# A fused decoder layer on one core: the shared expert's last 64 gates and ups computed as one product of 128 columns, and its down taken over 64 partitions

## The chip, the cores and the metric

The kernel runs on one core of one Trainium2 chip. The metric is the time of one execution on the device in microseconds. Times are given as the median of several executions. A second source is one profiled execution, whose trace names each instruction with its engine, its line in the kernel, its start and its duration. TensorE appears in the rows as PE (its weight loads as PEld), VectorE as DVE, ScalarE as ACT, GpSimd as POOL and SyncE, which issues most transfers, as SP.

## The reference, cut to what matters

One decoder layer over 8 sequences of 112 tokens (896 tokens) of width 512: causal self-attention, cross-attention to 375 context rows, and a feed-forward block, each on layer-normalised input and added to the residual. The change is in the last block:

```python
logits = x @ gate_w.T                       # 8 experts
probs = softmax(logits); top 2 of 8, normalised -> combine
g_sh = x @ shared_gate.T                    # I_SH = 2 * 352 = 704
u_sh = x @ shared_up.T
out = silu(g_sh) * u_sh @ shared_down.T     # shared expert, every token
g = einsum('nh,eih->nei', x, expert_gate)   # routed experts, I = 352
u = einsum('nh,eih->nei', x, expert_up)
y = einsum('nei,ehi->neh', silu(g) * u, expert_down)
out = out + einsum('neh,ne->nh', y, combine)
```

## The kernel before

**Numbers.** Every float32 product is done as three products of a 32-bit type that TensorE takes at full rate (fp32r): each operand is split into a high part (a ScalarE copy, `hi`) and a low part (source minus high part, mostly on VectorE, `low`), and `mm3` issues high by high, low by high and high by low (lines 512 to 514).

**The shared expert.** Its 704 hidden channels are padded to 768 and done in `NS = 6` chunks of 128; the last chunk holds 64 real channels and 64 of zeros. The tokens are done in two halves of `HT = 448`. For half `n` and chunk `c`, `up_pe(n, c, 0)` computes the gates and `up_pe(n, c, 1)` the ups, transposed (channels in the partitions, tokens in the columns): 4 contraction steps of 3 matmuls each, 448 columns, into a bank of PSUM. ScalarE applies silu to the gates into `sg` (`up_silu`), VectorE multiplies by the ups in PSUM (`up_mul`), ScalarE makes the high part of the result (`up_hi`, `hs`), VectorE the low part (`up_low`). The down contracts over the 128 channels of a chunk: for each of four tiles of 112 tokens, 3 matmuls of 512 columns.

**First half.** It runs on from the cross-attention: chunks 0 to 5 with `down_pe(c)`, which accumulates in four banks over all chunks. The weights of a chunk (1024 columns of gates and ups, 512 of the down) are loaded to `sf` and split in thirds (`s_hi_act(c, p)`, `s_low(c, p)`) into a ring of three buffers. Beside it VectorE works out the routing in a long row of small instructions. Its written order around the change is: `up_low(0, 3)`, `s_low(5, 0)`, `s_low(5, 1)`, normalised rows (`rows_normal`), `up_mul(0, 4)`, the experts' numbers, `up_low(0, 4)`, `s_low(5, 2)`, `up_mul(0, 5)`, `up_low(0, 5)`. TensorE's order is `up_pe(0, 5, 0)`, `up_pe(0, 5, 1)`, `down_pe(4)`, `down_pe(5)`.

**Second half and routed experts.** These are jobs: three shared jobs of two chunks each (0 and 1, 2 and 3, 4 and 5), and then 14 jobs of routed experts, which together have 21 blocks of 128 gathered rows. A job's weights come to a buffer `F[k % 2]`, and are split into `E[k % 2]`, part by part (`part_hi`, `part_low`), once the down of job `k - 2` has read that buffer. The down of a shared job is computed one job later: in the third job TensorE's order is `up_pe(1, 4, 0)`, `up_pe(1, 4, 1)`, the transposes of the first expert block (`turn_x`), the second job's down, `up_pe(1, 5, 0)`, `up_pe(1, 5, 1)`. The first expert block follows: `expert_up(0, 0)` (gates, 12 matmuls of 352 columns), the third job's down, `turn_x`, `expert_up(0, 1)`. In the shared down each of 4 token tiles gets 3 matmuls for the even chunk and 3 for the odd one.

In the third job VectorE's order is `up_mul(1, 4)`, the addition of the second job's result to the residual, `up_low(1, 4)`, the low part of the turned rows, the low parts of the first expert's gates and ups (`E_lo`, three parts), `up_mul(1, 5)`, `up_low(1, 5)`. ScalarE goes in the corresponding order.

Result banks of the gates and ups are handed out by a list of uses (`ups`), over four banks in rotation; `gu_wait` waits for the reader of the use before it in the same bank.

The tail: each expert block's result is added to the output by an indirect DMA of GpSimd, which waits for those of the job before.

Of the kernel before, what the change touches and what calls it, by code (L numbers as in the profile page):

```python
# [32 lines left out]
ISQ = 1.0 / float(DH) ** 0.5  # L33
LNE = 1e-5
SC = KC * 256 + D
NRB = -(-NT // BS)


# [42 lines left out]
def decoder_layer(nc, x_d, ctx_d, wqk_d, wv_d, wo_d, wqx_d, wkv_d, gw_d, moe_d, wexp_d, ident_d, mask_d, cst_d,  # L81
                  out_d):
    stack = ExitStack()
    with stack:
# [253 lines left out]

        def piece(k):

            last = (3, WU, WU + SC)
            if jobs[k][0] == "s":
                return (0, 0, SC), last
            return (0, 0, 940), (1, 940, 1880), (2, 1880, WU), last

        ups = [("u", 0, c, a) for c in range(4) for a in range(2)] + ["R"]
        ups += [("u", 0, c, a) for c in range(4, NS) for a in range(2)]
        t_uses, y_uses = [], []
        for n, (kind, j, k, _) in enumerate(its):
            prev = its[n - 1] if n else None  # L350
            ups += [("b", j, a) for a in range(2)] if kind == "e" else [("u", 1, 2 * j + q, a) for q in range(2) for a in range(2)]
# [98 lines left out]
        half_set = sig("half_set", [0])  # L450
        gl_done, lg_done = sig("gl_done", range(NB)), sig("lg_done", range(NB))

        third = [(c, p) for c in range(NS) for p in range(3)]
        s_hi, s_lo = sig("s_hi", third), sig("s_lo", third)
        g0_kept, u0_kept = sig("g0_kept", [0]), sig("u0_kept", [0])
        gu_full = sig("gu_full", ups)
# [51 lines left out]
        def tensor(e):  # L508
# [252 lines left out]
            def gu_wait(u):  # L761
                v = gu_before[u]
                if v[0] == "kn":
                    w.wait_ge(*kn_done[v[1]])
                elif v[0] == "oo":
                    w.wait_ge(*oo_done[v[1]])
                elif v[0] == "tx":
                    tx_free(v[1])
                elif v == "R":
                    w.wait_ge(*gu_dve["R"])  # L770
                elif v[:3] == ("u", 0, 0):
                    w.wait_ge(*(u0_kept if v[3] else g0_kept)[0])
                elif v[-1] == 0:
                    w.wait_ge(*gu_act[v[:-1]])
                else:
                    w.wait_ge(*gu_dve[v[:-1]])

            def up_pe(n, c, a):
                u, o = ("u", n, c, a), 0
                if n:  # L780
                    k = at_job["s", c // 2]
                    p, o = E[k % 2], WU if c % 2 else 0
                    part_wait(k, 3 if c % 2 else 0)
                else:
                    p = ring[c % 3] if c else SE
                    w.wait_ge(*s_lo[c, 1])
                w.wait_ge(*xT_done[3][4 * n + 3])
                gu_wait(u)
                for k in range(KC):
                    i = mm3(GU[u][:, 0:HT], at(p, ALL, toks(o + k * 256 + a * 128, 128)), at(xT, ALL, k, toks(n * HT, HT)),  # L790
                            k == 0, k == KC - 1)
                i.then_inc(*gu_full.did(u))

            def down_pe(c, tiles=range(4)):
                p = ring[c % 3] if c else SE
                w.wait_ge(*h_lo[0, c])
                w.wait_ge(*s_lo[c, 2])
                for b in tiles:
                    if c == 0:
                        if b == 1:  # L800
                            tx_free(tx_last[3])
                        else:
                            w.wait_ge(*x_exped[NK - 1, b])
                    i = mm3(AC[b][0:T, :], at(hs[c % 2], ALL, toks(b * T, T)), at(p, ALL, toks(1024, D)), c == 0, c == NS - 1)
                    i.then_inc(*ac_full.did((0, c, b)))

            def part_wait(k, p):
# [43 lines left out]
            def job_down(kind, j):  # L851
                k = job_of[j] if kind == "e" else at_job[kind, j]
                p = E[k % 2]
                if kind == "e":
                    u = (kind, j)
                    part_wait(k, 3)
                    w.wait_ge(*ht_lo[j])
                    y_wait(u)
                    for i, (o, n) in enumerate(IC):
                        z = WU + i * D  # L860
                        t = mm3(YB[u][:, :], (hT[j % 2][0][0:n, i, :], hT[j % 2][1][0:n, i, :]),
                                (p[0][0:n, z:z + D], p[1][0:n, z:z + D]), i == 0, i == 2)
                    t.then_inc(*y_full.did(u))
                    return
                w.wait_ge(*h_lo[1, 2 * j + 1])
                for t in range(4):
                    u = (kind, j, t)
                    y_wait(u)
                    for q in range(2):
                        i = mm3(YB[u][0:T, :], at(hs1 if q else hs[0], ALL, toks(t * T, T)), at(p, ALL, toks((WU if q else 0) + 1024, D)),  # L870
                                q == 0, q == 1)
                    i.then_inc(*y_full.did(u))

            def job_pe(n):
                kind, j, k, _ = its[n]
                prev = its[n - 1][0:2] if n else None
                nxt = its[n + 1] if n + 1 < len(its) else (None, 0)
                if kind == "e":
                    expert_up(j, 0)
                else:  # L880
                    up_pe(1, 2 * j, 0)
                if prev and prev[0] == "e":
                    turn_h(prev[1])
                elif prev and kind == "e":
                    job_down(*prev)
                if kind == "s":
                    up_pe(1, 2 * j, 1)
                    if k == 0:
                        up_pe(1, 2 * j + 1, 0)
                if nxt[0] == "e":  # L890
                    turn_x(nxt[1])
                if kind == "e":
                    expert_up(j, 1)
                if prev and (prev[0] == "e" or kind == "s"):
                    job_down(*prev)
                if kind == "s":
                    if k:
                        up_pe(1, 2 * j + 1, 0)
                    up_pe(1, 2 * j + 1, 1)

            last = NH // 2 - 1
            rows_pe(*keys[0])
# [45 lines left out]
            e.matmul(GU["R"][0:T, 64:72], tab[:, T:2 * T], small["cum"][:, 64:72], start=True, stop=True).then_inc(*gu_full.did("R"))  # L948
            down_pe(2, (2, 1))
            for c in (4, 5):  # L950
                for a in range(2):
                    up_pe(0, c, a)
                down_pe(c - 1)
            down_pe(NS - 1)
# [8 lines left out]
        def scalar(e):  # L963
# [243 lines left out]
            def up_silu(n, c):  # L1207
# [8 lines left out]
                elif n:  # L1216
                    w.wait_ge(*gu_dve[("u", 1, c - 2) if c > 1 else ("u", 0, NS - 1)])
                s_ = sg1 if n and c % 2 else sg[c % 2]
                silu(("u", n, c), ("u", n, c, 0), s_[:, :])

            def up_hi(n, c):
# [9 lines left out]
                hi(to[0][:, :], h_[:, :]).then_inc(*h_hi.did((n, c)))  # L1231

            def part_hi(k, p):
                for n, a, b in piece(k):
# [104 lines left out]
            s_hi_act(4, 2)  # L1339
            up_silu(0, 3)  # L1340
            s_hi_act(5, 0)
            s_hi_act(5, 1)
            up_hi(0, 3)
            s_hi_act(5, 2)
            part_hi(0, 0)
            up_silu(0, 4)
            up_hi(0, 4)
# [8 lines left out]
        def vector(e):  # L1356
# [264 lines left out]
                return (sg1, hh1, hs1) if n and c % 2 else (sg[c % 2], hh[c % 2], hs[c % 2])  # L1621

            def up_mul(n, c):
                g, h_ = ("u", n, c, 1), bufs(n, c)
                w.wait_ge(*gu_act["u", n, c])
                w.wait_ge(*gu_full[g])
                if n == 0 and c == 0:
                    w.wait_ge(*u0_kept[0])
                    e.tensor_tensor(h_[1][:, :], h_[0][:, :], h_[1][:, :], ALU.mult).then_inc(*gu_dve.did(("u", n, c)))
                    return  # L1630
                e.tensor_tensor(h_[1][:, :], h_[0][:, :], GU[g][:, 0:HT], ALU.mult).then_inc(*gu_dve.did(("u", n, c)))

            def up_low(n, c):
                h_ = bufs(n, c)
                w.wait_ge(*h_hi[n, c])
                low(h_[2][1][:, :], h_[1][:, :], h_[2][0][:, :]).then_inc(*h_lo.did((n, c)))

            def part_low(k, p):
                for n, a, b in piece(k):
# [221 lines left out]
            rows_normal(1)  # L1861
            up_low(0, 3)
            s_low(5, 0)
            s_low(5, 1)
            rows_normal(2)
            rows_normal(3)
            for b in range(4, NB):
# [11 lines left out]
            do(e.tensor_reduce(small["le2"][0:1, 0:NSL], le, X, ALU.add))  # L1879
            e.tensor_scalar(eid[:, :], small["le2"][0:1, 0:NSL], float(NE - 1), None, ALU.min).then_inc(*eid_done.did(0))  # L1880
            up_low(0, 4)
            s_low(5, 2)
            up_mul(0, 5)
            up_low(0, 5)
            part_low(0, 0)
# [128 lines left out]
        def sync(e):  # L2014
# [76 lines left out]
            def sf_load(c):  # L2091
                k = c - 2 if c > 3 else 0 if c == 1 else None
                if k is not None:
                    w.wait_ge(*s_lo[k, 2])
                e.dma_start((sf_e if c < 2 else sf[c % 2])[:, :], moe_d[c]).then_inc(*sf_in[c % 2].did(c))

            for n in range(4, NB * MC):
                ctx_load(n)
# [12 lines left out]
            def part_load(k, p):  # L2111
# [5 lines left out]
                        if (n == 3) == (p == 3):  # L2117
                            w.wait_ge(*e_lo[k - 2, n])
                elif k:
                    w.wait_ge(*s_lo[5, 2])  # L2120
                to = (Fd_in if p == 3 else Fu_in)[k % 2]
                if kind == "s":
                    o = WU if p == 3 else 0
                    e.dma_start(F[k % 2][:, o:o + SC], moe_d[2 * j + (p == 3)]).then_inc(*to.did(k))
# [115 lines left out]
```

## Time and profile before

| | |
|---|---|
| median of 3 runs | 971.27 us (970.53 to 971.85) |
| the profiled execution | 970.31 us |
| its span, first to last instruction | 968.50 us |
| TensorE busy | 927.6 us, 96% of the span |
| VectorE, ScalarE, GpSimd busy | 550.7, 455.3, 178.3 us |

An engine's busy share is an average over the whole span. What is idle and what ended the idle time is told by the timeline, in which an entry has square brackets if the engine sat idle before it. Matmuls are pipelined: an entry's duration is longer than the distance to the next one, and the distance is the cost in a saturated stretch.

### The profile page before, as it was taken

Reading aid. Unit: us, or ns where it says so; the run is one execution under the profiler, and the core shown is the slowest. Engines: PE = TensorE matmul, PEld = TensorE weight load, DVE = VectorE, ACT = ScalarE, POOL = GpSimd, SP = SyncE. Lnnn points to the kernel's source line nnn. Section 1 sums busy time; section 2 is a strip of 40 time slices with the busy share of each in tenths; the row PEclk is TensorE's granted clock in tenths of the full one; section 3 lists DMA queues with packets and bytes.
Section 4 is the critical chain, followed back from the end, with each engine's and each line's share of the span. In section 5 each row is a group of like instructions: output and inputs, shape, how many; then the busy total and the mean of one; then the engine's idle time right before and its main releaser. Section 6 shows DMA issues by size and latency. Waiting matters only on the chain.

```text
span 968.5 us, 17911 instructions
## 1 busy us (share of the span) xinstructions
PE 927.6 (96%) x7250; PEld 806.7 (83%) x7250; DVE 550.7 (57%) x1192; ACT 455.3 (47%) x1113; POOL 178.3 (18%) x137
## 2 busy tenths in 40 slices
PE   4999999999999999989999999999999999999994
PEld 3999999999999999867777777777778888899994
DVE  6254444444444445575645646555457756888882
ACT  3342424232323233536666656666575224665651
POOL 1220202020202022501011011011000710222222
PEclk9999999999999999999999999999999999999998
DMA  5110541010202003222201010010032684999983
GB/s 189 67 44 22 178 149 66 23 66 22 66 23 66 22 22 110 65 58 75 65 24 24 11 33 23 13 33 13 1 126 77 237 252 171 324 295 283 303 201 44
DMA packets 31329, 94.12 MB, mean 97 GB/s; under 512 B 6176, under 2 KB 9488, under 8 KB 29328
## 3 DMA queue, kind: packets, MB, share of 16 engines
q1 hardware_dynamic: 26944, 83.80, 25.7%
q0 software_dynamic: 4304, 9.19, 5.0%
q8 instruction: 57, 0.93, 0.4%
q14 instruction: 24, 0.20, 0.1%
HBM read 74.33 MB, written 16.81 MB: 94 GB/s over the span
## 4 chain that ended last, share of the span: by engine, by line
PE 89%; DVE 4%; ACT 3%; issue 1%; DMA 1%; POOL 1%; SPq 0%; DVEq 0%; ACTq 0%; POOLq 0%
PE bank L512 24%; PE bank L513 23%; PE bank L514 23%; PE bank L709 5%; PE bank L726 4%; PE bank L584 3%; PE bank L559 3%; PE bank L676 1%; ACT ee L1129 1%; PE bank L571 1%; PE bank L736 1%; PE bank L822 1%; PE bank L600 1%; DVE E_lo L1360 1%; DVE rt L1370 1%
## 5 line engine op out<-in xcount | busy, mean ns | idle before, releaser
L1129 ACT ACTIVATE ee<-bank 125x448 f32<-125x448 f32 x192 | 91.2, 549 | 21.2 <-PE bank L709 20.2
L512 PE MATMUL bank<-xT_hi,wqk_hi 128*128 128x448 f32 x256 | 95.6, 374 | 1.4 <-DVE xT_lo L1360 1.4
L514 PE MATMUL bank<-xT_lo,wqk_hi 128*128 128x448 f32 x256 | 93.4, 365 | 0.0
L513 PE MATMUL bank<-xT_hi,wqk_lo 128*128 128x448 f32 x256 | 93.3, 365 | 0.0
L512 PE MATMUL bank<-wkv_hi,ctx_hi 128*125 128x512 f32 x192 | 80.3, 418 | 3.0 <-DVE kn L1512 1.5
L1360 DVE TENSOR_TENSOR E_lo<-F,E_hi 128x940 fp32r<-128x940 f32 (+2 forms) x62 | 80.8, 1330 | 1.6 <-ACT E_hi L967 1.5
L513 PE MATMUL bank<-wkv_hi,ctx_lo 128*125 128x512 f32 x192 | 76.1, 396 | 0.0
L514 PE MATMUL bank<-wkv_lo,ctx_hi 128*125 128x512 f32 x192 | 75.7, 394 | 0.0
L512 PE MATMUL bank<-wv_hi,xT_hi 128*112 128x256 f32 x256 | 72.2, 282 | 0.0
L513 PE MATMUL bank<-wv_hi,xT_lo 128*112 128x256 f32 x256 | 71.7, 280 | 0.0
L514 PE MATMUL bank<-wv_lo,xT_hi 128*112 128x256 f32 x256 | 71.6, 280 | 0.0
L1903 POOL TENSOR_TENSOR ctx_lo<-ctx_f,ctx_hi 128x500 fp32r<-128x500 f32 x24 | 30.4, 1269 | 222.4 <-ACT ctx_hi L967 222.4
L1442 DVE TENSOR_TENSOR xa<-xa,bank 128x512 f32<-128x512 f32 x56 | 38.4, 687 | 53.3 <-PE bank L514 53.3
L967 ACT ACTIVATE E_hi<-F 128x940 fp32r<-128x940 f32 (+2 forms) x62 | 67.8, 1148 | 0.9
L2005 POOL DMA_INDIRECT out<-yg,meta x21 | 38.9, 1854 | 144.6 <-DMA out<-yg,meta 80.1
L1903 POOL TENSOR_TENSOR wqk_lo<-wqk_f,wqk_hi 128x1024 fp32r<-128x1024 f32 x16 | 37.8, 2360 | 145.8 <-ACT wqk_hi L967 145.8
L967 ACT ACTIVATE qk<-bank 128x448 f32<-128x448 f32 x32 | 17.4, 545 | 97.7 <-PE bank L514 97.7
L1026 ACT ACTIVATE pp<-sm,nm 112x112 f32<-112x112 f32 x128 | 48.1, 377 | 30.2 <-DVE nm L1414 30.2
L1521 DVE COPY kT<-bank 128x250 f32<-128x250 f32 x48 | 20.0, 416 | 68.8 <-PE bank L676 68.7
L512 PE MATMUL bank<-E_hi,xgT_hi 128*128 128x352 f32 x168 | 56.3, 335 | 0.6 <-DVE E_lo L1360 0.6
L1109 ACT ACTIVATE sq<-bank 125x256 f32<-125x256 f32 (+1 forms) x64 | 24.6, 384 | 63.3 <-PE bank L514 63.3
L514 PE MATMUL bank<-E_lo,xgT_hi 128*128 128x352 f32 x168 | 54.1, 322 | 0.0
(323 smaller groups left out, 2406.8 us busy)
## 6 DMA issues: line engine op xcount, KB each, us to landing
F<-wexp SPq DMA_DIRECT2D x14, 1408.0 KB, 8.1
F<-wexp SPq DMA_DIRECT2D x14, 768.0 KB, 7.4
wqk_f<-wqk SPq DMA_DIRECT2D x16, 512.0 KB, 3.3
ctx_f<-ctx SPq DMA_DIRECT2D x24, 250.0 KB, 2.7
slots<-zt SPq DMA_DIRECT2D x1, 5397.0 KB, 19.6
xg<-slots SPq DMA_DIRECT2D x21, 256.0 KB, 7.9
F<-moe SPq DMA_DIRECT2D x6, 768.0 KB, 7.7
wv_f<-wv SPq DMA_DIRECT2D x8, 512.0 KB, 3.6
```

The lines of the kernel that those rows point to most:

```text
L512: e.matmul(out, a[0], b[0], start=first, stop=False)
L513: e.matmul(out, a[1], b[0], start=False, stop=False)
L514: return e.matmul(out, a[0], b[1], start=False, stop=last)
L709: i = e.matmul(SX[r][0:MS, g * 2 * T:(g + 1) * 2 * T], kT[n % 6][32 * r:32 * r + 32, g, :], qT[u % 2][32 * r:32 * r + 32, g, :, :], start= ...
L726: i = e.matmul(AB[32 * c:32 * c + VW, r * T:(r + 1) * T], vb[n % 6][:, 8 * (c // 2) + 2 * r + c % 2, :], ee[(4 * n + r) % 8][:, c * T:(c + ...
L967: return e.activation(out, src, ACT.Copy)
L1026: i = e.activation(pp[g][:, c, :], sm[g][:, c, :], ACT.Exp, bias=nm[g][:, c:c + 1], scale=ISQ, accum_out=rs[g][:, c:c + 1])
L1129: e.activation(ee[(4 * n + r) % 8][:, :], SX[r][0:MS, 0:4 * T], ACT.Exp, scale=0.25).then_inc(*x_exped.did((n, r)))
L1360: return e.tensor_tensor(out, src, high.bitcast(F32), ALU.subtract)
L1442: e.tensor_tensor(xa[:, j, :], xa[:, j, :], PJ[u][:, :], ALU.add).then_inc(*pj_dve.did(u))
L1903: return e.tensor_tensor(out, src, high.bitcast(F32), ALU.subtract)
L2005: e.indirect_dma_start(out_d, bass.IndirectOffsetOnAxis(ap=meta[:, unit_of[j], 0:1].bitcast(U32), axis=0), yg[j % 4][:, :], None, compute_ ...
```

## The change

Chunk 5 has 64 gates and 64 ups. They are now one product: gates in result partitions 0 to 63, ups in 64 to 127. Silu reads the lower partitions and writes the upper ones of `sg`, and the product with the ups, the high and the low part work on partitions 64 to 127 alone. The down contracts over the upper 64 partitions. The weights of the chunk are 1024 columns in place of 1536, loaded and split in two parts in place of three. So `up_pe(0, 5, 1)` and `up_pe(1, 5, 1)` are gone, with one `s_hi_act` and one `s_low`, and `up_hi(0, 3)` stands before the second `s_hi_act` of chunk 5.

```diff
+LAST = 2 * D
-            last = (3, WU, WU + SC)
+            last = (3, WU, WU + (LAST if k == 2 else SC))
...
-        ups += [("u", 0, c, a) for c in range(4, NS) for a in range(2)]
+        ups += [("u", 0, 4, 0), ("u", 0, 4, 1), ("u", 0, 5, 0)]
...
-        third = [(c, p) for c in range(NS) for p in range(3)]
+        third = [(c, p) for c in range(NS) for p in range(3 if c < NS - 1 else 2)]
+        down_third = [2] * (NS - 1) + [1]
+        low_rows = slice(64, 128)
...
                 for k in range(KC):
-                    i = mm3(GU[u][:, 0:HT], at(p, ALL, toks(o + k * 256 + a * 128, 128)), at(xT, ALL, k, toks(n * HT, HT)),
-                            k == 0, k == KC - 1)
+                    z = o + (k * 128 if c == NS - 1 else k * 256 + a * 128)
+                    i = mm3(GU[u][:, 0:HT], at(p, ALL, toks(z, 128)), at(xT, ALL, k, toks(n * HT, HT)), k == 0, k == KC - 1)
...
-                w.wait_ge(*s_lo[c, 2])
+                w.wait_ge(*s_lo[c, down_third[c]])
+                part, z = (low_rows, D) if c == NS - 1 else (ALL, 1024)
...
-                    i = mm3(AC[b][0:T, :], at(hs[c % 2], ALL, toks(b * T, T)), at(p, ALL, toks(1024, D)), c == 0, c == NS - 1)
+                    i = mm3(AC[b][0:T, :], at(hs[c % 2], part, toks(b * T, T)), at(p, part, toks(z, D)), c == 0, c == NS - 1)
...
                     for q in range(2):
-                        i = mm3(YB[u][0:T, :], at(hs1 if q else hs[0], ALL, toks(t * T, T)), at(p, ALL, toks((WU if q else 0) + 1024, D)),
-                                q == 0, q == 1)
+                        part, z = (low_rows, D) if 2 * j + q == NS - 1 else (ALL, 1024)
+                        i = mm3(YB[u][0:T, :], at(hs1 if q else hs[0], part, toks(t * T, T)),
+                                at(p, part, toks((WU if q else 0) + z, D)), q == 0, q == 1)
...
-                    up_pe(1, 2 * j + 1, 1)
+                    if k < 2:
+                        up_pe(1, 2 * j + 1, 1)
...
-                for a in range(2):
+                for a in range(2 if c == 4 else 1):
                     up_pe(0, c, a)
                 down_pe(c - 1)
...
+                if c == NS - 1:
+                    g = "u", n, c, 0
+                    w.wait_ge(*gu_full[g])
+                    e.activation(s_[low_rows, :], GU[g][0:64, 0:HT], ACT.Silu).then_inc(*gu_act.did(("u", n, c)))
+                    return
...
             s_hi_act(5, 0)
+            up_hi(0, 3)
             s_hi_act(5, 1)
-            up_hi(0, 3)
-            s_hi_act(5, 2)
...
-                e.tensor_tensor(h_[1][:, :], h_[0][:, :], GU[g][:, 0:HT], ALU.mult).then_inc(*gu_dve.did(("u", n, c)))
+                e.tensor_tensor(h_[1][part, :], h_[0][part, :], GU[g][part, 0:HT], ALU.mult).then_inc(*gu_dve.did(("u", n, c)))
...
             s_low(5, 0)
-            s_low(5, 1)
...
             up_low(0, 4)
-            s_low(5, 2)
+            s_low(5, 1)
...
-                    w.wait_ge(*s_lo[5, 2])
+                    w.wait_ge(*s_lo[5, 1])
```

The transfers of chunk 5 are cut to `LAST` columns in both halves, and the host packs the weights accordingly.

## Rows read from the trace of the kernel before

**Rows 1.** The page: busy time, share of the span and number of instructions.

```profile
PE 927.6 (96%) x7250; PEld 806.7 (83%) x7250; DVE 550.7 (57%) x1192; ACT 455.3 (47%) x1113; POOL 178.3 (18%) x137
```

**Rows 2.** Busy time by stretches; the last three columns are granted clock, DMA share, GB/s.

```profile
758.30:766.20 7.90, 7.90 (x37) 6.40 (x36) 7.04 (x13) 1.95 (x3) 6.58 (x6) 1.00 0.78 219
766.20:802.40 36.20, 36.20 (x173) 31.30 (x173) 19.53 (x25) 10.31 (x13) 8.85 (x10) 1.00 0.89 304
824.10:953.60 129.50, 129.44 (x766) 120.18 (x767) 105.61 (x126) 74.31 (x104) 35.85 (x19) 1.00 0.88 264
```

**Rows 3.** Timeline of TensorE, first token half: start, duration in us, instruction.

```profile
755.88 0.36 PE L512 MATMUL bank<-xT_hi,S2hi 128*128 128x448 f32 x1
...
758.31 0.36 PE L512 MATMUL bank<-xT_hi,S2hi 128*128 128x448 f32 x1
...
760.74 0.39 PE L512 MATMUL bank<-S1hi,hs0hi 128*112 128x512 f32 x1
```

**Rows 4.** Timeline of VectorE, the same stretch.

```profile
752.69 1.29 DVE L1360 TENSOR_TENSOR S2lo<-sf,S2hi 128x512 fp32r<-128x512 f32 x2
753.90 2.83 DVE L1767 TENSOR_SCALAR rows<-xs,mv,rstd 112x512 f32<-112x512 f32 x6
...
759.76 0.60 DVE L1360 TENSOR_TENSOR hs0lo<-sg,hs0hi 128x448 fp32r<-128x448 f32 x1
760.29 0.67 DVE L1360 TENSOR_TENSOR S2lo<-sf,S2hi 128x512 fp32r<-128x512 f32 x1
...
762.27 0.63 DVE L1360 TENSOR_TENSOR hs_slo<-hh_s,hs_shi 128x448 fp32r<-128x448 f32 x1 [0.65 <-ACT hs_shi L967]
```

**Rows 5.** The chain that ended last, from the second shared job's down on.

```profile
802.71 0.58 ACT hs0hi L967
...
803.77 0.89 ACT E_hi L967
804.68 3.24 DVE E_lo L1360 x3
```

**Rows 6.** Timeline of TensorE where the routed experts begin.

```profile
808.12 0.40 PE L512 MATMUL bank<-E_hi,xgT_hi 128*128 128x352 f32 x1 [0.58 <-DVE E_lo L1360]
808.36 0.32 PE L513 MATMUL bank<-E_hi,xgT_lo 128*128 128x352 f32 x1
```

**Rows 7.** Timeline of TensorE, cross-attention scores over 32 partitions, opened at several points.

```profile
717.61 1.04 PE L709 MATMUL bank<-qT,kT 32*125 32x224 f32 x16
...
717.90 0.74 PE L709 MATMUL bank<-qT,kT 32*125 32x224 f32 x12
...
718.09 0.56 PE L709 MATMUL bank<-qT,kT 32*125 32x224 f32 x8
...
718.28 0.37 PE L709 MATMUL bank<-qT,kT 32*125 32x224 f32 x4
718.58 0.22 PE L512 MATMUL bank<-xT_hi,gw_hi 128*8 128x112 f32 x1
```

**Rows 8.** Timeline of TensorE, an expert's down over 96 partitions.

```profile
825.63 0.40 PE L512 MATMUL bank<-E_hi,hT0hi 96*128 96x512 f32 x1
...
826.33 0.32 PE L512 MATMUL bank<-E_hi,xgT_hi 128*128 128x352 f32 x1
```

**Rows 9.** Busy time by stretches after the last matmul; columns as in rows 2.

```profile
957.55:959.00 1.45, 0.00 (x1) 0.00 (x0) 0.75 (x1) 0.00 (x0) 0.00 (x0) 1.00 0.86 151
...
959.50:960.00 0.50, 0.00 (x0) 0.00 (x0) 0.00 (x0) 0.00 (x0) 0.00 (x0) 0.69 0.00 0
```

**Rows 10.** Timeline of TensorE at the first projection.

```profile
18.96 0.72 PE L512 MATMUL bank<-xT_hi,wqk_hi 128*128 128x448 f32 x1
...
20.60 0.57 PE L513 MATMUL bank<-xT_hi,wqk_lo 128*128 128x448 f32 x1
20.97 0.41 PE L514 MATMUL bank<-xT_lo,wqk_hi 128*128 128x448 f32 x1
```

More of the change, by code:

```diff
@@ L350, in decoder_layer @@
             prev = its[n - 1] if n else None
-            ups += [("b", j, a) for a in range(2)] if kind == "e" else [("u", 1, 2 * j + q, a) for q in range(2) for a in range(2)]
+            ups += [("b", j, a) for a in range(2)] if kind == "e" else [("u", 1, 2 * j + q, a) for q in range(2) for a in range(2) if 2 * j + q + a < NS]
             if prev and prev[0] == "e":
@@ L772, in gu_wait @@
                     w.wait_ge(*(u0_kept if v[3] else g0_kept)[0])
-                elif v[-1] == 0:
+                elif v[-1] == 0 and v[2:3] != (NS - 1,):
                     w.wait_ge(*gu_act[v[:-1]])
@@ L785, in up_pe @@
                     p = ring[c % 3] if c else SE
-                    w.wait_ge(*s_lo[c, 1])
+                    w.wait_ge(*s_lo[c, down_third[c] - 1])
                 w.wait_ge(*xT_done[3][4 * n + 3])
@@ L1230, in up_hi @@
                 h_, to = (hh1, hs1) if n and j else (hh[j], hs[j])
-                hi(to[0][:, :], h_[:, :]).then_inc(*h_hi.did((n, c)))
+                part = low_rows if c == NS - 1 else ALL
+                hi(to[0][part, :], h_[part, :]).then_inc(*h_hi.did((n, c)))
             def part_hi(k, p):
@@ L1623, in up_mul @@
             def up_mul(n, c):
-                g, h_ = ("u", n, c, 1), bufs(n, c)
+                g, h_ = ("u", n, c, 1 if c < NS - 1 else 0), bufs(n, c)
+                part = low_rows if c == NS - 1 else ALL
                 w.wait_ge(*gu_act["u", n, c])
@@ L1635, in up_low @@
                 w.wait_ge(*h_hi[n, c])
-                low(h_[2][1][:, :], h_[1][:, :], h_[2][0][:, :]).then_inc(*h_lo.did((n, c)))
+                part = low_rows if c == NS - 1 else ALL
+                low(h_[2][1][part, :], h_[1][part, :], h_[2][0][part, :]).then_inc(*h_lo.did((n, c)))
             def part_low(k, p):
@@ L2094, in sf_load @@
                     w.wait_ge(*s_lo[k, 2])
-                e.dma_start((sf_e if c < 2 else sf[c % 2])[:, :], moe_d[c]).then_inc(*sf_in[c % 2].did(c))
+                z = LAST if c == NS - 1 else SC
+                e.dma_start((sf_e if c < 2 else sf[c % 2])[:, 0:z], moe_d[c, :, 0:z]).then_inc(*sf_in[c % 2].did(c))
             for n in range(4, NB * MC):
@@ L2123, in part_load @@
                     o = WU if p == 3 else 0
-                    e.dma_start(F[k % 2][:, o:o + SC], moe_d[2 * j + (p == 3)]).then_inc(*to.did(k))
+                    z = LAST if k == 2 and p == 3 else SC
+                    e.dma_start(F[k % 2][:, o:o + z], moe_d[2 * j + (p == 3), :, 0:z]).then_inc(*to.did(k))
                 else:
@@ L2208 @@
     gw = inner(L0_ffn_gate_w)
-    up = np.zeros((2, NS * 128, D), np.float32)
-    up[0, :2 * NI] = np.asarray(L0_ffn_shared_gate)
-    up[1, :2 * NI] = np.asarray(L0_ffn_shared_up)
-    dn = np.zeros((NS * 128, D), np.float32)
-    dn[:2 * NI] = np.asarray(L0_ffn_shared_down).T
-    upc = inner(up.reshape(2, NS, 128, D).transpose(1, 0, 2, 3).reshape(NS, 256, D)).reshape(NS, 128, KC * 256)
-    moe = np.concatenate([upc, dn.reshape(NS, 128, D)], axis=2)
+    full = (NS - 1) * 128
+    up = np.stack([np.asarray(L0_ffn_shared_gate), np.asarray(L0_ffn_shared_up)])
+    dn = np.asarray(L0_ffn_shared_down).T
+    upc = inner(up[:, :full].reshape(2, NS - 1, 128, D).transpose(1, 0, 2, 3).reshape(NS - 1, 256, D)).reshape(NS - 1, 128, KC * 256)
+    moe = np.zeros((NS, 128, SC), np.float32)
+    moe[:NS - 1] = np.concatenate([upc, dn[:full].reshape(NS - 1, 128, D)], axis=2)
+    moe[NS - 1, :, :D] = inner(up[:, full:].reshape(128, D)).reshape(128, KC * 128)
+    moe[NS - 1, 64:, D:LAST] = dn[full:]
     eup = inner(np.concatenate([np.asarray(L0_ffn_expert_gate), np.asarray(L0_ffn_expert_up)], axis=1))
```

## The prediction, as made before the changed kernel ran

> **What bounds the kernel now.** I read the page first: TensorE is busy for 927.6 of 968.5 us [rows 1]. An average says nothing of one stage, so next came the busy time by stretches [rows 2]. From 758.3 to 802.4 us (the end of the first token half of the shared expert and two jobs of the second) TensorE is busy all the time, and so it is from 824.1 to 953.6. Between lies the passage from shared to routed experts, where it isn't. So a matmul saved in a saturated stretch shows only if what comes next is ready by then. Therefore I went to the two places where the change takes matmuls away, and read what the next TensorE instruction needs.
>
> One product of a chunk (12 matmuls of 448 columns) takes 758.31 - 755.88 = 2.43 us [rows 3], 0.20 each.
>
> **First token half: a product less.** The change removes product (5, ups) of tokens 0 to 447, at 758.31 to 760.74, straight before the down of chunk 4 [rows 3]. That down waits for `h_lo[0, 4]`. Its writer on VectorE starts at 759.76 and takes 0.60, so it ends at 760.36, only 0.38 us ahead of the down [rows 4]. Hence TensorE is free at 758.31 but VectorE sets the pace. VectorE works in program order from 752.7 on without an idle entry in these rows; what the change takes out ahead of that instruction is one of two `s_low` of chunk 5: 753.90 - 752.69 = 1.21 for the two, so 0.60 for one [rows 4]. New end 759.76. I add 0.15 from the end of the low part to the first matmul (in the row at 808.12 it is 0.20: the low parts end at 804.68 + 3.24 = 807.92 [rows 5, 6]) and 0.08 because a first matmul after a wait is longer (0.40 against 0.32 [rows 6]). The down of chunk 4 effectively starts at 759.99 instead of 760.74: a gain of 0.75, not 2.43; 1.6 us become a stall of TensorE.
>
> Its 12 matmuls of 512 columns take 12 x 0.233 = 2.80 us (three take 826.33 - 825.63 = 0.70 [rows 8]), until 762.8. The down of chunk 5 needs `h_lo[0, 5]`, before at 762.27 + 0.63 = 762.90 [rows 4]. Its chain (one `s_low`, the product with the ups, ScalarE's cast, the low part) is led by the same VectorE queue, so it moves by 0.60 to 762.3: no second stall, with 0.5 us of cover. Should that cover fail, each 0.1 us costs 0.1.
>
> **Second token half: a product less.** The change removes the last product of the third shared job, which ended in the stretch before 808.12. There TensorE is already waiting, 0.58 us, for VectorE's `E_lo` [rows 6]. The chain [rows 5] says for what: when the down of the second job ends (802.7), ScalarE casts `hs0hi`, `xgT_hi` and then the first expert's weight parts, and VectorE makes their low parts until 807.9. That expert's buffer is the one which the second job's down has just read, so the chain starts at the end of that down and at nothing else: 5.4 us whatever TensorE does meanwhile. TensorE used to cover it with two products; now it has one. The stall grows from 0.58 by 2.43 to about 3.0 us, and the second saving is worth 0. The down of the third job also keeps its place, since the product with the ups stands behind those low parts on VectorE.
>
> **Downs over 64 partitions.** Four tiles in the first half, four in the second, three matmuls each; column counts stay, so does the time for streaming. The trace has no such 64-partition matmul. Two rows bound what entering and leaving it costs. 96 partitions, same type: 0.70 us for three, as with 128, cost 0 [rows 8]. 32 partitions at offsets 0 to 96 [rows 7]: the first four matmuls take 717.90 - 717.61 = 0.29, the next four 718.09 - 717.90 = 0.19, so entry costs 0.10; the last four take 718.58 - 718.28 = 0.30, so leaving costs 0.11. The new matmul begins at partition 64, an offset that the 96-partition rows don't have and the 32-partition ones do, so I take 0.10. In the first half the four 64-partition tiles stand together: 2 changes. In the second each tile is a 128-partition group followed by a 64-partition one: 8 changes. 10 x 0.10 = 1.0 us, all in stretches that TensorE sets; bounds 0 and 10 x 0.2 = 2.0 (twice the row, for a load that isn't hidden either).
>
> The Trainium skill (TensorEngine Tiling (Array Packing), "Key Properties") states that changing the tiling mode drains the engine. It speaks against this change; by it the term above is real, without it zero, and rows 7 agree with it to the extent of those tenths. That page gives no time for it.
>
> **At nothing.** Elementwise work on the upper partitions has the same length per partition, so the same time. 256 KB less for chunk 5 in each half, one ScalarE cast less and shorter parts of job 2: all under TensorE's saturated stretch [rows 2]; VectorE's share in the first half is counted above. One use less in the ring of result banks shifts banks by one, and each use still waits for one that is four uses back. SyncE's load of job 1 waits for the low part that ends 0.6 earlier; nothing waits for it. `up_hi(0, 3)` now stands before the second cast, which no longer waits for a down; ScalarE's next work that somebody awaits is microseconds later. From 824.1 on everything shifts with TensorE.
>
> **Sum.** -0.75 + 0 + 1.0 = +0.25 us. Against the profiled execution (970.31: span 968.50 and 1.81 around it) that is 970.6; the median of the runs shown is 0.96 above that execution, so 971.5. About 0.2% (1.9 us) is what this kernel's measurement can tell from no change.
>
> **Rivals.**
> *No price for the 64 partitions.* For it: the 96-partition rows. Then -0.75: 970.5.
> *The clock falls in the longer stall (the slower side).* After the last matmul the granted clock is 1.00 in 957.55 to 959.00 and 0.69 in 959.50 to 960.00 [rows 9], the step from 2.4 to 1.2 GHz some 2 us after TensorE stopped, and TensorE had been idle once shortly before. A stall of 3.0 us is longer than that, though full work stands ahead of it. At the slow level a 448-column matmul takes 0.37 (20.97 - 20.60) instead of 0.20, from 18.96 to at least 20.97 [rows 10]: a loss of 1.0 us on 2 us of slow work. If the slow stretch is twice that, 2.0; if it lasted over the expert product and the whole third down (7.5 us), some 7. I take 2.0, for 971.27 + 0.25 + 2.0 = 973.5. It decides once the stall is long enough for the step; against it: the stall at 808 of 0.58 is far too short to show anything, and 3.0 is only just beyond the 2 us.
> The Trainium skill (TensorE: Matmul & The Clock Gate, "What's actually happening") says that the slow level is the default and activity lifts it; by that rule this rival would happen once the stall counts as idle.
> *Both products are saved in full.* 2 x 2.43 = 4.9: 966.4. That needs VectorE's chains to be no bound; rows 4 to 6 speak against it.
> *The DMA tail.* The last add to the output follows TensorE's end with transfers of some us; if they fall differently, +-1.5.
>
> **Chances.** Forecast (gain 0.75, changes of mode about 1.0) 0.42; no price 0.25; clock 0.18; both in full 0.05; tail or something else 0.10, split evenly. Faster by over 0.2% (below 969.3): 0.05 + a part of the tail, 0.07. Slower (above 973.2): most of the clock case and a part of the rest, 0.17. Within: 0.76. The range from 970.0 to 973.8 holds the first three cases with their bounds (0 to 2.0 for the mode, 1.0 to 2.2 for the clock) and leaves out the full saving and the long slow stretch. For the likeliest case alone 970.5 to 972.5.
>
> **What would show it.** Right: a TensorE wait of about 1.5 us before the down of chunk 4, released by `hs0lo`; a wait of about 3.0 before the first 128x352 product, released by `E_lo`, which still ends 5.2 us after the second job's down; the third down some 0.8 us longer than before at the same granted clock. Wrong: a third down as long as before (no price); a clock row below 1.00 after 805 us; or low parts of the expert's weights that don't follow the down, which would free the second product. The prediction goes wrong most easily in the size of the mode changes, as no row has this form, and in the clock.

## The result, and the profile of the changed kernel

The changed kernel is slower: 973.68 us (median of 9, 971.56 to 974.26) against 970.58 (median of 9) before, a ratio of 1.0029 with a 95% interval from 1.0018 to 1.0039, +3.1 us. The forecast was 971.5 with no measurable change; the measured time lies at the upper end of the range, where the rival with the falling clock had put it (973.5). The forecast was built on the median of 971.27 then known for the kernel before, 0.7 above the 970.58 of all nine executions; measured against that kernel, the upper end of the range was +2.5 us and the result is +3.1. The profiled execution took 973.01 with a span of 971.2.

The page's line of busy times answers to [rows 1]:

```profile
PE 927.3 (95%) x7226; PEld 803.6 (83%) x7226; DVE 549.1 (57%) x1191; ACT 454.1 (47%) x1112; POOL 180.1 (19%) x137
```

There are 24 matmuls fewer, and the engine's busy time is the same: what remained has become longer. Two lines of TensorE's waits from 700 us on (releaser: us in total, times, longest):

```profile
PE bank L516 <- DVE E_lo L1372: 4.6, 3, 3.0
PE bank L516 <- issue: 2.5, 2, 1.3
```

The first holds the wait of 3.0 us forecast before the first expert product. The second has one of 1.3 before the down of chunk 4; the profile names no releaser for it ("issue"), not `hs0lo` as forecast, and a reordering below tests what it waits for. Both stand in the timeline of TensorE, and with them what the engine does on resuming:

```profile
759.89 0.48 PE L516 MATMUL bank<-S1hi,hs0hi 128*112 128x512 f32 x1 [1.32 <-issue]
...
807.80 0.63 PE L516 MATMUL bank<-E_hi,xgT_hi 128*128 128x352 f32 x1 [3.04 <-DVE E_lo L1372]
808.23 0.50 PE L517 MATMUL bank<-E_hi,xgT_lo 128*128 128x352 f32 x1
808.52 0.50 PE L518 MATMUL bank<-E_lo,xgT_hi 128*128 128x352 f32 x1
...
810.58 0.40 PE L516 MATMUL bank<-E_hi,xgT_hi 128*128 128x352 f32 x1
810.81 0.32 PE L517 MATMUL bank<-E_hi,xgT_lo 128*128 128x352 f32 x1
```

From 808.2 to 810.6 the 352-column matmuls are 0.29 to 0.30 us apart and last 0.50; before, they last 0.32 [rows 6]. The stretches tell why (columns as in [rows 2]):

```profile
806.00:807.00 1.00, 0.00 (x0) 0.00 (x0) 1.00 (x2) 0.61 (x2) 0.00 (x0) 1.00 0.00 0
807.00:807.80 0.80, 0.00 (x0) 0.03 (x1) 0.77 (x2) 0.00 (x0) 0.00 (x0) 0.68 0.03 10
807.80:810.60 2.80, 2.80 (x10) 2.80 (x11) 1.07 (x2) 0.57 (x1) 0.00 (x0) 0.50 0.47 105
810.60:811.10 0.50, 0.50 (x4) 0.50 (x4) 0.00 (x0) 0.00 (x0) 0.00 (x0) 0.90 0.76 315
811.10:818.10 7.00, 7.00 (x27) 3.49 (x25) 2.06 (x3) 0.00 (x0) 0.00 (x0) 1.00 0.68 252
```

The granted clock stands at 1.00 until 807.0, falls inside the wait (at about 807.3), is 0.50 (1.2 in place of 2.4 GHz) while the first expert product runs, and is back at 810.7. TensorE's last matmul before the wait had ended at 804.76. The product takes 811.13 - 807.80 = 3.33 us; before it took 810.12 - 808.12 = 2.00: +1.33.

At 811.1 the clock is full again, and the third job's down is still long. A 128-partition group, a 64-partition group, and the start of the next:

```profile
811.60 0.39 PE L518 MATMUL bank<-E_lo,hs0hi 128*112 128x512 f32 x1
811.92 0.48 PE L516 MATMUL bank<-E_hi,hs_hi 64*112 64x512 f32 x1
812.24 0.39 PE L517 MATMUL bank<-E_hi,hs_lo 64*112 64x512 f32 x1
812.48 0.39 PE L518 MATMUL bank<-E_lo,hs_hi 64*112 64x512 f32 x1
812.80 0.49 PE L516 MATMUL bank<-E_hi,hs0hi 128*112 128x512 f32 x1
...
818.09 0.66 PE L827 MATMUL bank<-ident,xg 128*128 128x128 f32 x4
```

A matmul of 512 columns elsewhere comes 0.23 after the one before it. Here the first after a change comes 0.32 later (811.60 to 811.92, 812.48 to 812.80), and the one behind it again 0.32 (811.92 to 812.24). So each change costs 2 x 0.09 = 0.18 us, once on the way in and once behind the first matmul. The down takes 818.09 - 811.13 = 6.96 us against 5.53 before (810.12 to 815.65): +1.43, eight changes.

The sum along TensorE's timeline, changed minus before (two single executions, which can differ by some tenths of a us before the change begins: the last matmul of chunk 5's product starts at 757.7 in one kernel's trace below and at 758.3 in another's): -0.44 at the first product of the second token half (765.83 against 766.27), -0.32 at the first expert product, +1.01 at the third down, +2.44 behind it, +2.83 at the last matmul (959.98 against 957.15).

### The profile page after: what moved, and what is told of

Read it like the earlier page. It is cut to its first block, busy times and chain, and to the rows that moved or that the text cites. A ratio compares the mean times of both kernels' runs of the same rounds, so it can differ in the third digit from the quotient of the medians.

```text
span 971.2 us, 17862 instructions
## 1 busy us (share of the span) xinstructions
PE 927.3 (95%) x7226; PEld 803.6 (83%) x7226; DVE 549.1 (57%) x1191; ACT 454.1 (47%) x1112; POOL 180.1 (19%) x137
## 4 chain that ended last, share of the span: by engine, by line
PE 89%; DVE 5%; ACT 3%; issue 1%; DMA 1%; POOL 1%; SPq 0%; DVEq 0%; ACTq 0%; POOLq 0%
PE bank L516 24%; PE bank L517 23%; PE bank L518 23%; PE bank L713 5%; PE bank L730 4%; PE bank L588 3%; PE bank L563 3%; PE bank L680 1%; ACT ee L1136 1%; PE bank L575 1%; PE bank L740 1%; PE bank L827 1%; PE bank L604 1%; DVE E_lo L1372 1%; DVE rt L1382 1%
## 5 line engine op out<-in xcount | busy, mean ns | idle before, releaser
L1372 DVE TENSOR_TENSOR E_lo<-F,E_hi 128x940 fp32r<-128x940 f32 (+3 forms) x62 | 80.2, 1320 | 1.7 <-issue 0.8
L974 ACT ACTIVATE E_hi<-F 128x940 fp32r<-128x940 f32 (+3 forms) x62 | 67.3, 1139 | 0.9
L517 PE MATMUL bank<-E_hi,xgT_lo 128*128 128x352 f32 x168 | 54.6, 325 | 0.0
```

The lines of the kernel that those rows point to most:

```text
L517: e.matmul(out, a[1], b[0], start=False, stop=False)
L974: return e.activation(out, src, ACT.Copy)
L1372: return e.tensor_tensor(out, src, high.bitcast(F32), ALU.subtract)
```

## The experiments

All are timed with 11 executions, or as many as named, beside the kernel before on the same chip. "Full downs" means: chunk 5's downs contract over all 128 partitions; the lower 64 rows of its weights are zeros, so the result stays. "Before" in brackets is the median of the kernel before in the same session.

**The four corners: mode changes and clock.** First the changed kernel with full downs.

```diff
-                part, z = (low_rows, D) if c == NS - 1 else (ALL, 1024)
+                part, z = (ALL, D) if c == NS - 1 else (ALL, 1024)
...
-                        part, z = (low_rows, D) if 2 * j + q == NS - 1 else (ALL, 1024)
+                        part, z = (ALL, D) if 2 * j + q == NS - 1 else (ALL, 1024)
```

> The change, but both downs of chunk 5 contract over all 128 partitions; the weights of the lower 64 are zeros, so the result is the same. Theory (three terms: the mode changes cost about 0.18 us each, the clock's fall 1.3, the first half gives 0.5 to 0.75 back): the third job's down goes from 6.96 us to about 5.5 and the first half's last down from 3.0 to 2.8; 1.8 us less than the changed kernel, about 971.9. The stall of 3.0 us and the fall of the clock stay. Rival (64-partition groups cost nothing, all of the loss is clock and stall): no difference, 973.7.

Then the changed kernel with the second half's product done twice, to keep TensorE at work; the first copy is thrown away.

```diff
                 gu_wait(u)
+                for k in range(4 if n and c == NS - 1 else 0):
+                    mm3(GU[u][:, 0:HT], at(p, ALL, toks(o + k * 128, 128)), at(xT, ALL, k, toks(n * HT, HT)), k == 0, k == 3)
                 for k in range(KC):
```

> The change, but the product of chunk 5 in the second half is done twice (the first copy is overwritten), so that TensorE works in place of the long stall. Theory: the stall shrinks to about 0.6 us, the granted clock stays at 1.00 behind it, the first expert product takes 2.0 us instead of 3.3, and the kernel is 1.3 faster than the changed one, about 972.3, with a smaller spread between runs. Rival (the work itself was needed late, the clock is only a symptom): no gain, or a loss of 2.4 for the added product, 976.

Both edits:

> Both edits together: downs of chunk 5 over 128 partitions, product of chunk 5 in the second half done twice. If the three terms add up: 1.8 + 1.3 = 3.1 us less than the changed kernel, about 970.4, that is 0.1 to 0.7 below the kernel before. Rival (the two overlap, since the clock's fall lies next to the down): only 1.8 less, 971.9.

And the changed kernel as it is, again, to have all corners:

> The changed kernel again, unaltered, so that it stands on the same chip and in the same rounds as its variants. If the three terms add up, its gap to the kernel before is that of the variant with 128-partition downs (0.8) plus the mode changes (1.8), about 2.6 us; the four corners (with and without each of the two edits) would then be +2.6, +0.8, +1.0 and -0.7, nearly additive. Rival (the terms overlap): under 2.0.

| | no work added in the stall | product done twice |
|---|---|---|
| downs over 64 partitions | 973.36 (before 970.46) | 971.30 (before 970.26) |
| full downs | 971.06 (before 970.26) | 969.52 (before 970.26) |

Against the kernel before: +2.9, +1.0, +0.8, -0.7. Full downs take off 1.8 with the stall filled and 2.1 with it open; filling it takes off 1.5 with full downs and 1.9 with 64-partition ones. The 95% interval of each ratio is about 0.9 us to either side, so +0.8 and -0.7 alone are hardly told from no change; the differences of 1.5 to 2.1 along each side are larger and agree in both rows and both columns. Both causes are real, and nearly additive. Two of the expectations were somewhat low: filling the stall of the changed kernel took off 1.9 (1.3 expected), and its own gap was 2.9 (2.6 expected). The timeline of TensorE with full downs, the stall open:

```profile
807.49 0.40 PE L516 MATMUL bank<-E_hi,xgT_hi 128*128 128x352 f32 x1 [3.05 <-DVE E_lo L1372]
...
810.85 0.59 PE L516 MATMUL bank<-E_hi,hs0hi 128*112 128x512 f32 x1
...
816.57 0.60 PE L827 MATMUL bank<-ident,xg 128*128 128x128 f32 x4
```

The slow product stays (3.36 us); the down is back at 5.72, of which the first matmuls are still slow: together 1.55 us more than before (2.00 and 5.53). The granted clock in this trace, and in that of the changed kernel's second session, which had a wait of 3.05 up to 807.83:

```profile
804.50:807.80 3.30, 0.31 (x2) 0.34 (x3) 3.27 (x4) 1.80 (x3) 0.00 (x0) 1.00 0.01 2
807.80:811.20 3.40, 3.40 (x13) 3.36 (x12) 0.76 (x2) 0.57 (x1) 0.00 (x0) 0.51 0.65 195
...
804.80:807.80 3.00, 0.00 (x0) 0.00 (x0) 2.97 (x4) 1.84 (x3) 0.00 (x0) 1.00 0.01 3
807.80:811.20 3.40, 3.37 (x12) 3.40 (x13) 1.10 (x2) 0.57 (x1) 0.00 (x0) 0.50 0.50 136
```

The clock is low for 3.4 us in both, as in the first trace (807.3 to 810.7), but here it falls only at the end of the wait (807.8 in the second session) or behind it: with full downs about 0.35 us after the matmuls had resumed at 807.49. In the first trace 0.5 us of the slow stretch lie in the wait, where they cost nothing. That is why the same stretch costs 1.33 there and 1.55 in these two (in the second session the product takes 3.55 and the down 6.94).

With 64-partition downs and the stall filled:

```profile
807.27 0.40 PE L516 MATMUL bank<-E_hi,xgT_hi 128*128 128x352 f32 x1 [0.58 <-DVE E_lo L1374]
...
809.27 0.44 PE L516 MATMUL bank<-E_hi,hs0hi 128*112 128x512 f32 x1
...
816.28 0.66 PE L829 MATMUL bank<-ident,xg 128*128 128x128 f32 x4
```

The other way round: the product takes 2.00, the down 7.01. It also shows that 12 matmuls more in front of the expert product don't delay it: it starts at 807.27 with them and at 807.80 without, and the two executions are 0.5 us apart already at the start of the down of chunk 4 (759.37 and 759.89). That is the second saving, worth 0.

**Half of the product done twice** (6 extra matmuls, full downs).

> 128-partition downs, and only half of the product of chunk 5 in the second half is done twice (6 matmuls more), so the stall is about 1.8 us. Theory (the clock falls only if TensorE stood still long enough, 2.5 us in the changed kernel's trace): no fall, the same time as with the whole product done twice, about 0.7 below the kernel before. Rival (any stall over about 1.5 us brings it in some of the runs): a spread over two levels 1.4 us apart, median between.

969.87 (before 970.46), -0.6 by the medians, but the ratio is 1.0000 (0.9991 to 1.0009), so no gain over the kernel before is shown. In the profiled execution the wait is 1.81 us and the product takes 2.00. Nine of the eleven executions lie between 969.34 and 970.35 with a mean granted clock of 0.996; two lie at 971.87 and 972.20 with 0.994. So the theory seems to hold for most executions and the rival for two of them (these two have no trace, so that their clock fell at this place is inferred): where the border lies is not settled, and whether the clock falls is not fixed by the kernel alone.

**Is it the number of partitions or their offset?** The kernel before, whose chunk 5 has its real channels in the lower 64 partitions, with the downs of that chunk over these alone.

```diff
+                    part = slice(0, 64) if c == NS - 1 else ALL
-                    i = mm3(AC[b][0:T, :], at(hs[c % 2], ALL, toks(b * T, T)), at(p, ALL, toks(1024, D)), c == 0, c == NS - 1)
+                    i = mm3(AC[b][0:T, :], at(hs[c % 2], part, toks(b * T, T)), at(p, part, toks(1024, D)), c == 0, c == NS - 1)
...
+                        part = slice(0, 64) if 2 * j + q == NS - 1 else ALL
-                        i = mm3(YB[u][0:T, :], at(hs1 if q else hs[0], ALL, toks(t * T, T)), at(p, ALL, toks((WU if q else 0) + 1024, D)),
+                        i = mm3(YB[u][0:T, :], at(hs1 if q else hs[0], part, toks(t * T, T)), at(p, part, toks((WU if q else 0) + 1024, D)),
```

> The kernel before, with one edit: the downs of chunk 5 contract over partitions 0 to 63 alone (the other 64 channels are the padding of zeros, so the result is the same). No work is removed from the products, nothing is reordered, the stall stays at 0.58 us. Theory (going from a 128-partition to a 64-partition group and back costs about 0.18 us each way, whatever the offset): the third down takes 6.95 us in place of 5.53, the first half's last down some 0.35 more, and the kernel is 1.8 us slower than before. Rival (only the offset of 64 costs; groups that begin at partition 0 are free like the 96-partition ones): no difference.

972.43 (before 970.58), +1.85, with the ratio between 1.0010 and 1.0028. The timeline of its TensorE in the third down:

```profile
811.33 0.39 PE L514 MATMUL bank<-E_lo,hs0hi 128*112 128x512 f32 x1
811.64 0.48 PE L512 MATMUL bank<-E_hi,hs_hi 64*112 64x512 f32 x1
811.97 0.40 PE L513 MATMUL bank<-E_hi,hs_lo 64*112 64x512 f32 x1
812.21 0.39 PE L514 MATMUL bank<-E_lo,hs_hi 64*112 64x512 f32 x1
812.53 0.48 PE L512 MATMUL bank<-E_hi,hs0hi 128*112 128x512 f32 x1
```

The same 0.31 to 0.33 us on each side of a change. The third down takes 6.92 us, against 6.96 with the groups at partition 64. The offset plays no part; the change of group size alone does, and it costs the whole 1.8 us without any stall or slow clock beside it.

**The first half's saving.** Full downs, and VectorE makes the operands of the two downs before the small instructions that number the experts.

```diff
             up_mul(0, 4)
+            up_low(0, 4)
+            s_low(5, 1)
+            up_mul(0, 5)
+            up_low(0, 5)
+            part_low(0, 0)
+            part_low(0, 3)
             le, le2 = (small[i][0:1, :].rearrange("p (j e) -> p j e", e=NE) for i in ("le", "le2"))
...
             e.tensor_scalar(eid[:, :], small["le2"][0:1, 0:NSL], float(NE - 1), None, ALU.min).then_inc(*eid_done.did(0))
-            up_low(0, 4)
-            s_low(5, 1)
-            up_mul(0, 5)
-            up_low(0, 5)
-            part_low(0, 0)
-            part_low(0, 3)
```

> Downs of chunk 5 over 128 partitions, and in the first half VectorE makes the operands of the downs of chunks 4 and 5 before the small instructions that number the experts. Theory (the first half's saving is lost to VectorE's order): TensorE goes on without the stall of 1.3 us before the down of chunk 4, and the kernel is 1.5 us faster than the one with downs over 128 partitions alone, about 970.4. Rival (something else, such as the weights' low parts or the second down's operand, takes the place of that wait): under 0.5 of it arrives.

The timeline of its TensorE, from the last matmul of chunk 5's product on:

```profile
758.12 0.36 PE L518 MATMUL bank<-xT_lo,S2hi 128*128 128x448 f32 x1
758.32 0.39 PE L516 MATMUL bank<-S1hi,hs0hi 128*112 128x512 f32 x1
...
761.17 0.49 PE L516 MATMUL bank<-S2hi,hs_shi 128*112 128x512 f32 x1
...
764.05 0.37 PE L516 MATMUL bank<-xT_hi,E_hi 128*128 128x448 f32 x1
```

No wait before the down of chunk 4; the second half starts at 764.05 instead of 765.65. In time: 969.81 against 971.06 with full downs alone, -1.25 of the 1.5 expected (no saving against the kernel before is shown by this alone: 0.9989 to 1.0007). VectorE's order was what kept the first saving.

In this kernel's profiled execution (968.34) the wait before the expert product was 3.05 us as before, and the clock did not fall:

```profile
803.00:806.00 3.00, 0.02 (x1) 0.00 (x0) 2.97 (x4) 1.88 (x3) 0.00 (x0) 1.00 0.01 3
806.00:808.00 2.00, 1.93 (x12) 1.96 (x13) 1.13 (x2) 0.57 (x1) 0.00 (x0) 1.00 0.40 73
```

The expert product took 2.00. Two of its eleven executions have a mean granted clock of 0.996 (968.34, 968.99), nine have 0.993 to 0.995 (969.50 to 971.04). The changed kernel divides likewise: of its twenty executions in two sessions four have 0.996 or 0.997 (970.68 to 971.56), sixteen 0.992 to 0.995 (972.64 to 974.35). The third digit is a hint and no proof: 0.995 also occurs, rarely, in kernels without a wait over 1.4 us, and the profiled execution of the kernel before has it, with a clock of 1.00 from 20 to 950 us. The mean contains the fall after the last matmul too (there the last 8.8 us of the span, in the changed kernel's trace the last 6.9), and the difference of 1.9 us between these two is more than half of the 3.4 us that the fall in the middle adds. For the changed kernel the times themselves leave a gap of 1.1 us between the two groups.

**The second saving.** Full downs, and in the third job the second job's down goes between the gates and the ups of chunk 4. ScalarE and VectorE, which would otherwise wait for those ups, do the expert's weight parts first.

```diff
# TensorE
-                if kind == "s":
+                if kind == "s" and k < 2:
                     up_pe(1, 2 * j, 1)
...
                 if prev and (prev[0] == "e" or kind == "s"):
                     job_down(*prev)
                 if kind == "s":
+                    if k == 2:
+                        up_pe(1, 2 * j, 1)
# ScalarE, and up_mul and up_low of VectorE in the same way
-                    up_hi(1, 2 * j)
+                    if k < 2:
+                        up_hi(1, 2 * j)
...
                     for i in splits(n, 0):
                         part_hi(*i)
+                    if k == 2:
+                        up_hi(1, 2 * j)
```

> 128-partition downs, and in the third shared job TensorE does the second job's down between the gates and the ups of chunk 4, so that two products stand behind that down instead of one; ScalarE and VectorE take up the chunk's product with the ups after the expert's weight parts. Theory (the second saving is lost because the chain of the expert's weights hangs on the end of that down): the stall before the first expert product goes from 3.0 to about 0.3, no fall of the clock; a new wait of some 0.5 for the third down's operand may appear; the kernel is about 3.5 us faster than with 128-partition downs alone, 967.5. Rival (the weights' parts hang on something else, their load for example): no gain.

968.52 (before 970.46), -1.9, and 2.7 less than full downs alone, each against its own kernel before (3.5 less was expected). Its timeline:

```profile
804.35 0.32 PE L516 MATMUL bank<-E_hi,xgT_hi 128*128 128x352 f32 x1
...
807.82 0.49 PE L516 MATMUL bank<-E_hi,hs0hi 128*112 128x512 f32 x1 [1.39 <-DVE hs_lo L1377]
```

The stall before the expert product is gone, 3.1 us earlier than with full downs alone. But a new one of 1.4 us, not 0.5 as expected, stands before the third down.

**Both reorderings**, full downs:

> 128-partition downs and both reorderings (first half and third job). Theory: the two savings of 2.4 us each arrive, less some tenths for new waits; 970.26 of the kernel before less 4.3, about 966.0. Rival (the transfers at the end or the expert stage give part of it back): 967 or more.

966.98 (6 executions; before 970.46), -3.5, and in a second session:

> Both reorderings with 128-partition downs again, beside the next kernel on the same chip: 3.5 us below the kernel before.

966.93 (5 executions; before 970.58), -3.65. The wait before the third down is 1.38 in both sessions. VectorE's timeline (first session) shows a chain taken twice, with a gap for ScalarE's cast each time:

```profile
802.82 0.61 DVE L1649 TENSOR_TENSOR sg<-sg,bank 128x448 f32<-128x448 f32 x1
804.08 0.63 DVE L1377 TENSOR_TENSOR hs0lo<-sg,hs0hi 128x448 fp32r<-128x448 f32 x1 [0.65 <-ACT hs0hi L976]
804.74 0.62 DVE L1649 TENSOR_TENSOR hh<-sg,bank 64x448 f32<-64x448 f32 x1
806.00 0.62 DVE L1377 TENSOR_TENSOR hs_lo<-hh,hs_hi 64x448 fp32r<-64x448 f32 x1 [0.64 <-ACT hs_hi L976]
```

**The chains interleaved.**

```diff
# VectorE, third job
                     if k == 2:
                         up_mul(1, 2 * j)
-                        up_low(1, 2 * j)
                     up_mul(1, 2 * j + 1)
+                    if k == 2:
+                        up_low(1, 2 * j)
# ScalarE, third job
+                    up_silu(1, 2 * j + 1)
                     if k == 2:
                         up_hi(1, 2 * j)
-                    up_silu(1, 2 * j + 1)
```

> As the kernel with both reorderings, but in the third job VectorE does the two products with the ups one after the other and then the two low parts, and ScalarE's silu of chunk 5 stands before the casts. Theory (the new wait of 1.4 us before the third down is the chain product, cast, low part taken twice in a row on VectorE): the wait falls to about 0.3, and the kernel is 1.1 us faster than the one before it, 4.6 below the kernel before. Rival (the wait is for something else, or is given back at the next stall): no difference.

966.07 (5 executions; before 970.58), ratio 0.9957 with an interval from 0.9943 to 0.9970: -4.5, and 0.9 below the kernel with both reorderings (1.1 expected; five executions of each). The wait fell to 0.67 (0.3 expected):

```profile
804.86 0.48 PE L516 MATMUL bank<-E_hi,hs0hi 128*112 128x512 f32 x1 [0.67 <-DVE hs_lo L1377]
```

This is the fastest kernel of the study. It keeps the changed kernel's single product and has neither the 64-partition groups nor the two stalls. The reorderings were not tried on the kernel before, without the saved products. By its trace there was little for them to win there: no wait in the first half, 0.58 us before the expert product.

## Why the prediction was right and where it was not

The range of 970.0 to 973.8 holds the measured 973.68, but the forecast case (+0.25 us) didn't happen. What happened is the rival with the falling clock, which had a chance of 0.18, and a mode term near its upper bound. That the rival's 973.5 lies so close is luck in part: its base was 0.7 us too high and its price of the mode changes 0.8 too low.

**First half: a gain of 0.75 in place of 2.43.** Right. The down of chunk 4 starts at 759.89, 0.85 earlier than in [rows 3], behind a wait of 1.3 us (1.6 forecast), and its second matmul 0.74 earlier (760.22 against 760.96). The reordering on VectorE gave the rest back. VectorE's low part starts at 759.24:

```profile
752.78 0.68 DVE L1372 TENSOR_TENSOR S2lo<-sf,S2hi 128x512 fp32r<-128x512 f32 x1
753.38 2.82 DVE L1781 TENSOR_SCALAR rows<-xs,mv,rstd 112x512 f32<-112x512 f32 x6
...
759.24 0.60 DVE L1372 TENSOR_TENSOR hs0lo<-sg,hs0hi 128x448 fp32r<-128x448 f32 x1
```

against 759.76 in [rows 4]: one `S2lo` less and nothing else. Its end at 759.84 is 0.05 before the down starts. There is no wait before the down of chunk 5, as forecast.

**Second half: a gain of 0.** Right, and shown from both sides: adding the work back moves nothing but the clock, moving the down forward frees it.

**The price of the 64-partition groups: 10 x 0.10 = 1.0.** This term of the sum was mis-sized: the ten changes cost 1.8 us (1.8 by the filled pair of kernels, 1.85 by the kernel before with its downs narrowed). I had read from [rows 7] one side of each change: on entering the time behind the first matmuls (0.10), on leaving the time before the next group (0.11). Each change costs that twice, 0.09 before the first matmul of the new size and 0.09 behind it. The reason I gave for the 32-partition rows as the nearest, the offset, was wrong, although it led to the nearer row: groups at offset 0 pay the same. The upper bound of 2.0 held.
The Trainium skill (TensorEngine Tiling (Array Packing), "Key Properties") says that a change of tiling mode drains the engine; the trace agrees in that every change here costs 0.18 us, though it doesn't show a drain as such, and the 96-partition groups, which cost nothing [rows 8], are in line with it if they count as the full size.

**The clock.** The forecast took the case in which it stays; it fell, in both profiled executions of the changed kernel and, by their times and mean granted clocks, in sixteen of twenty. That is the step of the prediction that failed: a stall of 3.0 us was judged "only just beyond" what [rows 9] show. The clock fell 2.5, 3.0 and 3.4 us after TensorE's last matmul had ended in the three traces that have the fall (changed kernel, its second session, full downs). In a fourth, with the same wait of 3.05, it didn't fall. The price of 2.0 is more than the 1.33 and 1.55 us of the traces and the 1.5 of the pair with full downs, about the 1.9 of the pair with 64-partition downs, and less than the 2.6 between the two groups of executions of the changed kernel (medians of 971.1 and 973.7).

**The sum.** -0.75, +1.8 and +1.3 to 2.0 make +2.4 to 3.1; measured +3.1. About 0.4 of the trace's +2.83 at the last matmul comes after the third down, where both kernels run the same instructions. Half of it is a wait that the kernel before doesn't have:

```profile
916.44 0.40 PE L516 MATMUL bank<-E_hi,xgT_hi 128*128 128x352 f32 x1 [0.19 <-DVE E_lo L1372]
```

The rest isn't explained. From the end of the third down to the last matmul the kernel before took 141.50 us, and the twelve other profiled executions 141.84 to 142.11, even that of the kernel before with narrowed downs (141.84). Why the fall costs up to 2.6 between groups of executions stays open. Both profiled executions of the changed kernel (973.01 and 973.52) belong to the slower group, and their traces show 1.33 and 1.55; no execution of the faster group was profiled.

## What to carry to other kernels

Before matmuls are taken out of a saturated stretch, ask what the next instruction waits for: here both savings ran into chains of VectorE, which could be read off the trace and removed by reordering. With the reorderings the saving is worth 4.5 us in all, while the saving alone was worth none. A wait that grows is not neutral: of four profiled executions with a wait of 3.0 us three had the lower clock behind it, and filling the wait with work that is thrown away took off 1.5 to 1.9 us. And a contraction over half of the partitions saved nothing here, as the 512 columns set the time (0.23 us a matmul either way); padding with zeros to the size of the neighbours cost nothing, changing the size cost 0.18 us each time.

## What the runs showed of the hardware that was not expected

A change between 128-partition and 64-partition matmuls costs 0.09 us before the first and 0.09 behind the first matmul of the new size, at offset 0 as at 64. The granted clock fell in some executions of a kernel and not in others, at equal waits (3.05 us: full clock in the profiled execution of one kernel, 0.50 behind it in that of another), and with a wait of 1.8 us two of eleven executions have a lower mean clock and a longer time. The stretch at the lower level (0.50) lasted 3.4 us in each of the three traces that have it, and began 0.5 us before the end of the wait in one, at its end in the second and about 0.35 us behind it in the third, so its price was 1.33 to 1.55 us.
